# The routing table of a mixture-of-experts kernel from bf16 products of exact parts, with one VectorE operation per choice

## The reference

```python
scores = softmax(xt @ Wg.T)                       # [2048, 16]
gmask  = the 2 best of 4 groups of 4 experts, by their largest score
topi   = top_k(where(gmask, scores, -inf), 4)     # 4 experts per token
weights = scores at topi
h = silu(einsum('td,eid->eti', xt, W1)) * einsum('td,eid->eti', xt, W3)
y = einsum('etd,te->td', einsum('eti,edi->etd', h, W2), combine)   # combine holds weights at topi
z = silu(xt @ Ws1.T) * (xt @ Ws3.T) @ Ws2.T       # shared experts, all tokens
out = x + tanh(g_ffn) * (y + z)
```

## Time and profile before

| | |
|---|---|
| median of 3 runs | 1331.7 us (1331.23 to 1332.85) |
| profiled execution | 1331.93 us, span 1330.1 us |
| TensorE matmul busy | 1261.9 us, 95% of the span |
| VectorE busy | 659.6 us, 50% |
| ScalarE, GpSimd busy | 587.1 us, 639.0 us |
| mean granted TensorE clock | 0.981 |
| shared stage | about 528 to 757 us of the span |
| routing tables on TensorE | 596.8 to 671 us |

### The profile page before, as it was taken

One profiled execution on the slowest core, in us unless ns is written; L12 is line 12 of the kernel. 1 busy time (PEld: TensorE's weight loads), 2 busy tenths in 40 slices (PEclk: granted clock), 3 DMA queues, 4 the chain that ended last, 5 costly groups with the idle time before them and its releaser, 6 DMA issues. The chain is left out here.

```text
span 1330.1 us, 27215 instructions
## 1 busy us (share of the span) xinstructions
PE 1261.9 (95%) x8457; PEld 923.6 (69%) x8458; DVE 659.6 (50%) x1862; ACT 587.1 (44%) x1018; POOL 639.0 (48%) x726
## 2 busy tenths in 40 slices
PE   7998999999997998999999899999999999999995
PEld 4554544444443345777777589999999999999994
DVE  5345788898896656766424033332353343343300
ACT  1222566666665223321223145555555455555552
POOL 6000333333333323442536256666667766767664
PEclk8998999999998999999999999999999999999998
DMA  9452333333333604000013235555666566665443
GB/s 342 153 161 94 102 109 97 111 93 105 100 108 93 193 32 190 29 36 32 32 40 121 89 73 128 143 136 139 143 144 137 137 155 174 143 158 138 78 72 40
DMA packets 73870, 152.92 MB, mean 115 GB/s; under 512 B 10725, under 2 KB 16357, under 8 KB 73049
## 3 DMA queue, kind: packets, MB, share of 16 engines
q1 hardware_dynamic: 52776, 102.37, 23.5%
q0 software_dynamic: 21040, 49.88, 18.4%
HBM read 97.56 MB, written 52.23 MB: 113 GB/s over the span
## 5 line engine op out<-in xcount | busy, mean ns | idle before, releaser
L208 DVE CUSTOM_DVE_ANT_0 a_mb<-a_mb,late 128x128 f32<-128x128 f32 (+3 forms) x512 | 244.5, 510 | 51.1 <-PE a_mb L189 44.5
L1511 DVE CAST e_w<-e_w 128x480 fp32r<-128x480 f32 x135 | 76.5, 567 | 304.0 <-DMA e_w<-in_w2T 299.8
L640 ACT ACTIVATE a_at<-a_eb 128x1024 f32<-128x1024 f32 (+3 forms) x256 | 179.7, 705 | 103.2 <-PE a_eb L702 102.7
L576 POOL TENSOR_SCALAR_AFFINE_SELECT a_at<-a_at 128x256 f32<-128x256 f32 x256 | 106.0, 415 | 226.1 <-ACT a_at L640 225.9
L1663 PE MATMUL e_yps<-e_w,e_hT 128*128 x711 | 197.3, 404 | 0.9 <-ACT e_hT L1574 0.9
L1642 PE MATMUL e_up<-e_w,e_xT 128*128 x948 | 171.4, 330 | 0.0
L1642 PE MATMUL e_gate<-e_w,e_xT 128*128 x948 | 169.1, 327 | 1.0 <-issue 1.0
L1642 PEld LDWEIGHTS e_gate<-e_w,e_xT 128*128 128x128 f32 x948 | 157.3, 190 | 10.5 <-issue 5.6
L1642 PEld LDWEIGHTS e_up<-e_w,e_xT 128*128 128x128 f32 x948 | 150.6, 190 | 0.0
L1663 PEld LDWEIGHTS e_yps<-e_w,e_hT 128*128 128x128 f32 x711 | 128.1, 189 | 25.5 <-issue 1.2
L189 PE MATMUL a_mb<-a_k,a_q 49*128 49x256 f32 (+2 forms) x512 | 121.1, 426 | 18.7 <-DVE a_mx L208 8.6
(11 more groups left out here) (243 smaller groups left out, 1766.3 us busy)
## 6 DMA issues: line engine op xcount, KB each, us to landing
e_w<-in_w13T SPq DMA_DIRECT2D x16, 1408.0 KB, 6.2
dq<-p_parts SPq DMA_DIRECT2D x32, 256.0 KB, 2.4
a_q<-dq SPq DMA_DIRECT2D x64, 128.0 KB
do<-a_o SPq DMA_DIRECT2D x32, 256.0 KB, 2.1
e_w<-in_w2T SPq DMA_DIRECT2D x16, 512.0 KB, 5.6
a_k<-dk SPq DMA_DIRECT2D x64, 98.0 KB
e_w<-in_ctxT SPq DMA_DIRECT2D x4, 1024.0 KB, 13.8
e_w<-in_x SPq DMA_DIRECT2D x4, 1024.0 KB, 13.5
```

The costliest lines, as they stand in the source:

```text
L208: eng.tensor_tensor_reduce(out=b[:, 0:w], in0=b[:, 0:w], in1=io["late"][:, SEQ - w:SEQ], scale=1.0, scalar=3 * NEG, op0=ALU.add, op1=ALU.m ...
L576: eng.affine_select(out=square, in_=square, compare_op=ALU.is_ge, fill=0.0, base=0, pattern=[[0, 2], [1, P]], channel_multiplier=-1).then_ ...
L640: eng.activation(at[r % 2][:, ch, 2 * hp:2 * hp + 2, ch * P:SEQ], eb[hp][:, :, ch * P:SEQ], ACT.Exp, scale=0.25).then_inc(s_exp, 1)
```

## The change

Both numbers of a choice are split into bf16 parts whose sum is exact enough: two for token minus row (`puts` parts 1 and 3), three for the weight (parts 0, 2 and 4). Part n is the rest rounded to bf16, and the rest is reduced by it. `at_row` and `at_col` become bf16, `at_col` with five parts of 79 columns (395). `at_tile` and its semaphore go. For each of a block's four choices one `scalar_tensor_tensor` compares the tile numbers with the choice's tile and multiplies by its five parts. The table's products become bf16, 128 x 395, into five columns of `tokps`, which VectorE adds up at the end. The rests, `topf` and `puts` move into memory that is in use already.

```diff
-        NG, NK = E // EG, TOPK
+        NG, NK, PARTS = E // EG, TOPK, 5
...
-        top, topi, topf = sb("r_top", [P, NT, 8]), sb("r_topi", [P, NT, 8], mybir.dt.uint32), sb("r_topf", [P, NT, 8])
+        top, topi = sb("r_top", [P, NT, 8]), sb("r_topi", [P, NT, 8], mybir.dt.uint32)
+        topf = io["rows"][2][:, 384:].rearrange("p (t k) -> p t k", t=NT)
...
-        at_row = [io["rows"][2 + r].rearrange("p (k n) -> p k n", k=NK) for r in range(2)]
-        at_tile = sb("r_attile", [P, NK, TILES])
-        at_col = [sb(f"r_atcol{r}", [P, NK, 2, TILES]) for r in range(2)]
-        put = sb("r_put", [P, NT, NK, 2])
+        at_row = [io["rows"][2 + r].bitcast(BF16)[:, 0:NK * P].rearrange("p (k n) -> p k n", k=NK) for r in range(2)]
+        at_col = [sb(f"r_atcol{r}", [P, NK, PARTS, TILES], BF16) for r in range(2)]
+        put = io["rows"][2][:, 256:384].rearrange("p (t k n) -> p t k n", t=NT, k=NK)
+        puts = z[:].rearrange("p t e -> p (t e)").bitcast(BF16)[:, 0:NT * NK * PARTS].rearrange("p (t k n) -> p t k n", t=NT, k=NK)
...
-        tokps = ps("r_tokps", [P, 2 * TILES])
+        tokps = ps("r_tokps", [P, PARTS, TILES])
...
-            eng.tensor_scalar(put[:, :, :, 1], top[:, :, 0:NK], tg[:, 0:1], None, ALU.mult).then_inc(s_v, 1)
+            eng.tensor_scalar(put[:, :, :, 0], top[:, :, 0:NK], tg[:, 0:1], None, ALU.mult).then_inc(s_v, 1)
...
-            eng.tensor_tensor(put[:, :, :, 0], rows(tok[:].rearrange("p (t o) -> p t o", o=1), NK), row[:], ALU.subtract).then_inc(s_v, 1)
-            eng.wait_ge(s_v, next(done))
+            eng.tensor_tensor(put[:, :, :, 1], rows(tok[:].rearrange("p (t o) -> p t o", o=1), NK), row[:], ALU.subtract).then_inc(s_v, 1)
+            eng.wait_ge(s_v, next(done))
+            for n in range(PARTS):
+                rest = put[:, :, :, n % 2]
+                eng.tensor_copy(puts[:, :, :, n], rest).then_inc(s_v, 1)
+                eng.wait_ge(s_v, next(done))
+                if n + 2 < PARTS:
+                    eng.tensor_tensor(rest, rest, puts[:, :, :, n], ALU.subtract).then_inc(s_v, 1)
+                    eng.wait_ge(s_v, next(done))
...
-                if t:
-                    eng.wait_ge(s_row, 3 * t + 1)
-                eng.tensor_tensor(at_tile[:], iota_g[:].rearrange("p (o g) -> p o g", o=1).broadcast_to([P, NK, TILES]),
-                                  col[:, t, :].rearrange("p (k o) -> p k o", o=1).broadcast_to([P, NK, TILES]), ALU.is_equal).then_inc(s_tile, 1)
-                eng.wait_ge(s_tile, t + 2)
-                for n in range(2):
-                    eng.tensor_tensor(at_col[r][:, :, n, :], at_tile[:],
-                                      put[:, t, :, n:n + 1].broadcast_to([P, NK, TILES]), ALU.mult).then_inc(s_row, 1)
+                for k in range(NK):
+                    eng.scalar_tensor_tensor(out=at_col[r][:, k], in0=iota_g[:].rearrange("p (o g) -> p o g", o=1).broadcast_to([P, PARTS, TILES]),
+                                             scalar=col[:, t, k:k + 1], in1=puts[:, t, k, :].rearrange("p (n o) -> p n o", o=1).broadcast_to([P, PARTS, TILES]),
+                                             op0=ALU.is_equal, op1=ALU.mult).then_inc(s_row, 1)
...
-            eng.tensor_scalar(indexf[:], tokps[:, 0:TILES], pad[:, 0:1], None, ALU.add).then_inc(s_v, 1)
+            eng.tensor_scalar(indexf[:], tokps[:, 1, :], pad[:, 0:1], None, ALU.add).then_inc(s_v, 1)
+            eng.wait_ge(s_v, next(done))
+            eng.tensor_tensor(indexf[:], indexf[:], tokps[:, 3, :], ALU.add).then_inc(s_v, 1)
...
-            eng.tensor_copy(io["scale"], tokps[:, TILES:]).then_inc(s_v, 1)
-            eng.wait_ge(s_v, next(done))
+            eng.tensor_copy(scale, tokps[:, 0, :]).then_inc(s_v, 1)
+            eng.wait_ge(s_v, next(done))
+            for n in (2, 4):
+                eng.tensor_tensor(scale, scale, tokps[:, n, :], ALU.add).then_inc(s_v, 1)
+                eng.wait_ge(s_v, next(done))
...
-                eng.wait_ge(s_row, 3 * t + 4)
+                eng.wait_ge(s_row, (NK + 1) * (t + 1) + 1)
                 for k in range(NK):
-                    mm = eng.matmul(tokps[:], at_row[r][:, k, :], at_col[r][:, k].rearrange("p n g -> p (n g)"), start=t == 0 and k == 0,
+                    mm = eng.matmul(flat(tokps[:]), at_row[r][:, k, :], at_col[r][:, k].rearrange("p n g -> p (n g)"), start=t == 0 and k == 0,
```

More of the change, by code:

```diff
@@ L1049, in stage_shared @@
         row, col = sb("r_row", [P, NT, NK]), sb("r_col", [P, NT, NK])
-        at_row = [io["rows"][2 + r].rearrange("p (k n) -> p k n", k=NK) for r in range(2)]
-        at_tile = sb("r_attile", [P, NK, TILES])
-        at_col = [sb(f"r_atcol{r}", [P, NK, 2, TILES]) for r in range(2)]
-        put = sb("r_put", [P, NT, NK, 2])
+        at_row = [io["rows"][2 + r].bitcast(BF16)[:, 0:NK * P].rearrange("p (k n) -> p k n", k=NK) for r in range(2)]
+        at_col = [sb(f"r_atcol{r}", [P, NK, PARTS, TILES], BF16) for r in range(2)]
+        put = io["rows"][2][:, 256:384].rearrange("p (t k n) -> p t k n", t=NT, k=NK)
+        puts = z[:].rearrange("p t e -> p (t e)").bitcast(BF16)[:, 0:NT * NK * PARTS].rearrange("p (t k n) -> p t k n", t=NT, k=NK)
         pad_i, pad = sb("r_padi", [P, 1], I32), sb("r_pad", [P, 1])
-        indexf = sb("r_indexf", [P, TILES])
+        indexf, scale = sb("r_indexf", [P, TILES]), io["scale"]
         tile_e, tile_b = sb("r_tilee", [1, TILES]), sb("r_tileb", [1, TILES])
@@ L1065, in stage_shared @@
         ready, expert = sb("r_ready", [1, TILES], I32), sb("r_expert", [1, TILES], I32)
-        s_row, s_tile, s_tok = sem("r_srow"), sem("r_stile"), sem("r_stok")
+        s_row, s_tok = sem("r_srow"), sem("r_stok")
         weights = shared_weights(io)
@@ L1088, in _ @@
         def _(eng):
-            begin(eng, s_c, s_ch, s_v, s_row, s_tile, s_high, s_low)
+            begin(eng, s_c, s_ch, s_v, s_row, s_high, s_low)
             done = itertools.count(2)
@@ L1146, in _ @@
                 eng.wait_ge(s_v, next(done))
-            eng.tensor_copy(topf[:], topi[:]).then_inc(s_v, 1)
+            eng.tensor_copy(topf, topi[:]).then_inc(s_v, 1)
             eng.wait_ge(s_v, next(done))
             eng.wait_ge(s_tg, 2)
-            eng.tensor_scalar(put[:, :, :, 1], top[:, :, 0:NK], tg[:, 0:1], None, ALU.mult).then_inc(s_v, 1)
+            eng.tensor_scalar(put[:, :, :, 0], top[:, :, 0:NK], tg[:, 0:1], None, ALU.mult).then_inc(s_v, 1)
             eng.wait_ge(s_v, next(done))
```

## The result

| | before | after |
|---|---|---|
| median of four runs each, us | 1331.47 | 1339.74 (1337.36 to 1340.47) |
| ratio | | 1.0056, interval 1.0035 to 1.0077 |
| span of the profiled execution | 1330.1 | 1337.4 |
| VectorE busy | 659.6 | 682.4 |
| mean granted TensorE clock | 0.981 | 0.975 |

The kernel is 8.3 us slower. The page of the changed kernel shows it against the earlier trace rows: TensorE's busy time is the same, its share is lower.

A forecast was written before the change was run, and what follows sets the result against it. TensorE, busy 95% of the span, was taken to bound the kernel. Products -6.1, waits +9.1 and clock +3.0 made +6.0 us over 1331.7, forecast 1337.6 us, range 1330.5 to 1341.5.

The forecast's parts named there:

- Products: TensorE's table products: eight one-pass bf16 products of 395 columns, 178 ns each, save 0.76 us a group, 6.1 in all.
- VectorE per table: Building a table on VectorE: 0.60 us plus four new operations of 0.555, 2.82 us; two tables 5.70, before 3.9.
- GpSimd: VectorE's table building: each GpSimd operation on SBUF that it meets costs VectorE 1.05 us, also with the new operations.
- The new order: Table groups: VectorE late every other group, TensorE waits 2.27 us before the second table, four times, 9.1 us lost.
- The clock: TensorE behind the four longer waits: granted clock falls twice, 1.5 us each, 3.0 us lost; bounds none and four of 1.69.
- The discount for hidden parts: In the clock term: a little of each fall is hidden where VectorE comes late anyway, so 1.5 us each.
- Cover: Ahead of the tables: VectorE's added work and GpSimd meetings, together 6.0 us, cost nothing under its 10.78 us of idling.
- Rival 4: Table groups: 0.60 us an operation, waits of 2.45 us, all four followed by clock falls of 1.69: 1342.2 us; chance 0.12.
- Rival 2: Table groups: scalar free, two tables under 4.8 us, six waits of 1.0 us against 6.1 saved, no fall: 1331.6; chance 0.17.
- Rival 1: Table building: GpSimd doesn't hold up the new operations, VectorE keeps up, all 6.1 us kept: 1325.6 us; chance 0.11.
- rival 3: Table groups: waits as in the forecast, but no wait lets TensorE's clock fall: 1334.7 us; chance 0.25.
- Rival 5: Table products: two passes of 0.34 us each, a group dearer by 0.6 us; chance inside that of Rival 4.

The follow-up runs named there:

- the repetition: The changed kernel run again as it is, with a second profile: 1338.91 us, ratio 1.0057 to the kernel before.
- the idle products: Changed kernel plus 14 or 7 unused bf16 products on TensorE ahead of the second table of groups 2, 4, 6, 8: 1331.01 and 1332.04 us.

## Why the prediction was right, and where it was off

It forecast 1337.6 us, slower, with waits in every other group; 1339.74 was measured, within the range. By its steps:

- **Products.** 178 ns forecast, 176 measured; 6.1 us saved forecast, 6.2 measured.
- **VectorE per table.** 559 + 60 ns forecast for one operation, 617 (shortest) to 624 (median) measured; 0.555 us from start to start forecast, (2.25 - 0.62) / 3 = 0.54 measured.
- **GpSimd.** 1.05 us lost at each meeting forecast, 3.27 - 2.25 = 1.02 and (4.33 - 2.25) / 2 = 1.04 measured. The open point, whether this form of operation stands still too, is decided by the 4.33 us row. The rule of the Trainium skill (SBUF — State Buffer, "Who interferes with whom") says that a VectorE instruction with two SBUF inputs contends with a GpSimd instruction that reads SBUF. The trace agrees for this form: four operations took 4.33 us beside two GpSimd operations and 2.25 us without one. With one GpSimd operation fewer in each unit the stretch is 131.02 us, against 139.2 with the waits and the full clock.
- **The new order.** Waits in groups 2, 4, 6, 8 and none in the others, as forecast, down to the third GpSimd operation that falls before the pair's end: it was forecast 7.80 us behind the group's start and came at 7.79 (603.94). Each wait was forecast at 2.27 us and measured at 2.10, 0.7 us too much in all.
- **The clock** is the term that was mis-sized: two falls of 1.5 us, 3.0, against 6.1 measured. There were three falls in the profile, and the one over the down products cost 2.9. In the repetition two falls cost the same 6.0, one of them 4.4 us. The discount for hidden parts was wrong: right behind a wait neither engine has a lead, so a slow clock makes TensorE the later of the two, and VectorE then waits for it. The row at 667.87 shows this: VectorE waits 2.15 us for the products behind the slow block, where it waited 0.53 at the same place of the first half (612.84), and TensorE's next wait is 1.95 us as ever. Each 1.6 us came out in full.
- **Cover.** VectorE's lead ahead of its third block fell from 10.78 to 3.35 us, 7.4 used where I counted 6.0. What is behind the tables shifted as a whole: the first product of the expert stage came 7.7 us later (765.81 for 758.10), and the span is 7.3 us longer.
- **Luck.** That the time came within 2.1 us of the forecast is in part luck: the waits were 0.7 us too long and the clock 3.1 too cheap, which partly cancels. The count of falls was drawn from one case in two and not from a mechanism, and it was three in one profile and two in the other.
- **Slips in the sums.** The sum of +6.0 over 1331.7 is 1337.7, not 1337.6. Before, VectorE made the next two tables in 5.70 us (598.07 to 603.77), not 5.6. Rival 4's wait with 0.60 us an operation is 2.27 + 8 x 0.045 = 2.63 us, not 2.45, so its time is 1342.9. Rival 2's first condition isn't enough: with a free scalar two tables take 2 x (0.60 + 4 x 0.49) + 0.06 = 5.18 us, over the 4.76 that it asks for. None of these changes the forecast by more than 0.1 us.

Rival 1 (VectorE keeps up) fell with the 4.33 us rows; rival 2 (balance) with the waits; rival 3 (full clock) is what the idle products made, 1331.01 and 1332.04 us in place of its 1334.7; the shorter waits are 0.7 of the gap, and the rest lies outside the stretch. Rival 4 had the cost of the falls nearly right (6.8 against 6.1, but by four falls) and the waits too long. Rival 5 fell with 176 ns.

## What to carry to other kernels

When a change moves work from the engine that bounds to one with slack, work out the slack between two deadlines, not from the busy share: here VectorE was busy half of the time and had 1.9 us to give in 7.6, and each GpSimd operation on SBUF took 1 us of them. If the helper had a lead, count the buffers that let it keep it; a third one turned 8 us lost into 7 us gained (5.9 by the stretch). And price a wait on TensorE above its length where it comes near 2 us, since the clock may fall behind it, as it did in five of eight cases here. Waits of up to 1.55 us in the same stretch, and waits with idle products in them, had no such price; the closing stage has one fall behind 1.51 us.

## What the runs showed that I had not expected

The clock's part is as large as three of the four waits. All falls in the stretch followed a standstill of 1.94 or 1.95 us; with 1.18 (four times), 1.22 and 1.55 us none did, though the closing stage shows one behind 1.51 us and none behind another of 1.51. Why five of eight equal waits were followed by a fall and three weren't stays open, and so does why one fall lasted 3 us longer than another. The common part ahead of the tables varied by 7 us between profiles of the same TensorE instructions. The clock has a share in that: from 20 to 40 us of the span it was 0.85 in the profile before and 1.00 in that of the version with three buffers and four parts. With effects of 2 us it was the stretch in the trace, which repeats within about 0.1 us, that settled the terms, and not the medians.
